# Attention with heads of 16 columns: projections of the next batch earlier in the order, heads issued in pairs, and score products on 64-row halves of the array

## The chip, the cores and the metric

One core of a Trainium2 chip runs one launch of the whole model. The metric is device time in microseconds (us). The core's engines are TensorE (PE in the rows; its weight loads PEld), VectorE (DVE), ScalarE (ACT), GpSimd (POOL) and SyncE (SP), which issues the DMAs here. Each runs its own list of instructions in order and waits on semaphores.

## The reference

Four layers, each a gated attention block and a gated mixture of experts, on 8 batches of 256 rows and 256 columns. The attention of layers 1 and 2 has 16 heads of 16 columns. With x the state, c the context:

```
n = layernorm(x)
q, k, v = n @ Wq + bq, c @ Wk + bk, c @ Wv + bv          # split into 16 heads of 16
layer 1: q, k = rotary(q), rotary(k); causal and padding masks
s = q @ k.T / 4 + mask
p = softmax(s)
x = x + tanh(gate) * (concat(p @ v) @ Wo + bo)
```

Layer 2 has no rotation and no causal mask. Layers 0 and 3 have other attention code.

## The kernel before, in words

`small_phase` (L1697) is the attention of layers 1 (`att1`, `rotary` true) and 2 (`att2`); layers 0 and 3 and the experts are not touched. The 8 batches times 16 heads are 128 steps. In step s TensorE does four things in this order: `scores` of head s+8 (L1823 to L1825 in layer 1, L1828 in layer 2), from which VectorE's `largest` (L2016) takes each row's maximum; `shifted` of head s (L1842 to L1844, L1847), the same product transposed, from which the maximum is taken off by an additional row of the operands and of which ScalarE takes the exponential (`weights_of`, L1952); the rounds of this step; and `values` of head s−1 (L1871). Scores, shifted products and outputs have two banks each, the exponentials three buffers.

The operands of a head are fp32 numbers split into high and low parts, laid side by side into 64 rows: `lay_hi` on ScalarE (L1962) and `lay_lo` on VectorE (L2030) write `qs` and `ks`, which TensorE transposes in four parts of four heads, qT and kT (L1910). ScalarE evacuates qT into `QT` (L1975), VectorE kT into `KT` (L2069). `KT` has two heads in its 128 rows. `QT` has a copy for each of the two, in which the other head's 64 rows are zero, so that each product goes over 128 rows; GpSimd's `clear` (L2166) writes the zeros at the start.

The `plan` table gives each round of batch b its step, 16(b−1) + the table's number: nT (transposes of the normalized input, L1893), q, k, v and out (projections, L94 to L96, as three products of split operands), qT and kT with their parts, mt (transposed maxima, L1914, which ScalarE copies and SyncE's DMAs put into `QT`), and OT (transposed outputs, L1918). All rounds share two banks in the order of the table. The first scores of batch b are at its number 8, its first shifted products at 16. The text counts the steps from 16(b−1), the number 0 of batch b, for other batches' rounds too: the out round of batch b−2 is at 4 there, kT part 3 of batch b−1 at −1. `lay_hi` and `lay_lo` of a batch are at its numbers 0 (q) and 2 (k).

GpSimd's list is, for each batch b: `norm(b)` (L2127), `aux(b)` (L2136, L2137: mask columns into `qs` and `ks`, which waits for kT part 3 of batch b−1), in layer 1 `rotate` of q and then k (L2146 to L2155), and `add_bias(b-2)` (L2161), which waits for VectorE's sum behind the output projection (L2076). `normalize` (L2038, L2043) divides eight heads' outputs.

Of the kernel before, what the change touches and what calls it, by code (L numbers as in the profile page):

```python
# [24 lines left out]
P = 128  # L25
B = 8
# [1670 lines left out]
def small_phase(nc, G, I, name, layer, weights, w, mask, biases, rotary):  # L1697
# [8 lines left out]
    plan = [(-4, "nT", 0), (-3, "q", 0), (-2, "k", 0), (1, "v", 0), (3, "qT", 0), (5, "kT", 0), (6, "qT", 1), (7, "kT", 1),  # L1706
            (8, "qT", 2), (10, "kT", 2), (11, "qT", 3), (15, "kT", 3), (13, "mt", 0), (17, "mt", 1), (21, "mt", 2), (25, "mt", 3),
            (26, "OT", 0), (34, "OT", 1), (36, "out", 0)]
    ROUNDS = sorted(((16 * (b - 1) + at, kind, b, part) for b in range(B) for at, kind, part in plan), key=lambda r: r[0])
    POS = {r[1:]: i for i, r in enumerate(ROUNDS)}  # L1710
    ON_ACT = ("qT", "mt")
# [8 lines left out]
    def batch_at(s, at):  # L1720
        b = (s - at) // 16 + 1
        return b if (s - at) % 16 == 0 and 0 <= b < B else None

    with ExitStack() as ctx:
# [10 lines left out]
        if rotary:  # L1735
# [5 lines left out]
            r1, r2 = sb("turn1", [P, TB, D]), sb("turn2", [P, TB, D])  # L1741
# [21 lines left out]
        n_ready, aux_done, f_raw, f_ready, laid_hi, laid_lo = (sem(n) for n in ("n_ready", "aux_done", "f_raw", "f_ready", "laid_hi", "laid_lo"))  # L1763
# [8 lines left out]
        def both(bank):  # L1772
            return bank[:, :].rearrange("p (c s) -> p c s", c=2)

# [3 lines left out]
        with nc.Block() as block:  # L1778
            @block.sync
            def _(sp):  # L1780
# [17 lines left out]
                for s in range(FIRST, LAST):  # L1798
                    for kind, b, part in rounds_at(s):
                        if kind == "mt":  # L1800
                            n = 4 * b + part
                            sp.wait_ge(mt_done, n + 1)
                            for e in range(2):
                                sp.dma_start(QT[b % 2][64 * e + 49:64 * e + 50, e, 2 * part:2 * part + 2, :].bitcast(F32),
                                             mT[n % 2][4 * e:4 * e + 4, :].bitcast(F32)).then_inc(row_in, 16)
# [4 lines left out]
            def _(pe):  # L1810
                def scores(s):
# [5 lines left out]
                    if s == H:  # L1817
                        pe.wait_ge(cleared, 2)
                    if s >= 2:
                        pe.wait_ge(m_done, s - 1)  # L1820
                    bank, q, k = s_ps[s % 2], QT[b % 2], KT[b % 2]
                    if rotary:
                        pe.matmul(bank[:, P:3 * P], ident16[:, :], tri[:, :, :], start=True, stop=False, skip_group_check=True)  # L1823
# [8 lines left out]
                def shifted(s):  # L1832
# [3 lines left out]
                    if s >= 2:  # L1836
                        pe.wait_ge(e_done, s - 1)
# [706 lines left out]
```

## Time and profile before

| | us |
|---|---|
| three runs | 3793.33, 3807.78, 3793.79; median 3793.79 |
| profiled execution | 3807.24, span 3805.2 |
| TensorE busy over the span | 2787.3 (73%) |
| VectorE, ScalarE, GpSimd busy | 2549.3, 1615.5, 1634.2 |
| attention of layer 1 | about 701 to 1092 |
| attention of layer 2 | about 1677 to 1979 |

In the rows the names of buffers stand without their numbers, "out<-in" is written and read, and x is a count. The time in square brackets is how long the engine was idle before the row and which engine and line released it. PEclk is the clock that TensorE was granted as a share of 2.4 GHz; 0.50 is 1.2 GHz.

### The profile page before, as it was taken

What the parts mean: (1) busy time and instruction counts of PE and PEld (TensorE: products, weight loads), DVE (VectorE), ACT (ScalarE), POOL (GpSimd) and SP (SyncE); (2) the same over time, 40 slices, a digit from 0 to 9 for tenths busy, and PEclk for the clock granted to TensorE, in tenths of its full rate; (3) what the DMA queues carried; (4) which work ended last, traced back from release to release, by engine and by line L of the source; (5) the groups of instructions that cost most, each with busy time, mean ns of one, the idle gap of its engine ahead of it and who ended that gap; (6) DMA issues with size and microseconds to landing.
All of it is one profiled execution on the core that took longest, in us unless ns stands there. A gap on an engine that the chain in (4) does not pass through costs nothing. (4 is left out here: it accounts for less than half of the span.)

```text
span 3805.2 us, 66554 instructions
## 1 busy us (share of the span) xinstructions
PE 2787.3 (73%) x20707; PEld 2610.0 (69%) x20708; DVE 2549.3 (67%) x4818; ACT 1615.5 (42%) x3415; POOL 1634.2 (43%) x1281
## 2 busy tenths in 40 slices
PE   5663584288867999929972788886189998498883
PEld 4551574288856999929971677776189888298883
DVE  4664597544436999955642788887567666388886
ACT  3222352133324555515531344443267666265551
POOL 0102455522203488740003666665344443317775
PEclk9786798677768999969965999999599999699997
DMA  3032686100005655530001455553200000365554
GB/s 96 23 133 100 197 248 182 52 18 12 7 30 202 209 195 200 171 97 18 18 4 70 150 156 158 157 156 117 67 12 6 11 11 1 127 208 180 189 182 126
DMA packets 244577, 408.83 MB, mean 107 GB/s; under 512 B 26656, under 2 KB 136492, under 8 KB 244384
## 3 DMA queue, kind: packets, MB, share of 16 engines
q1 hardware_dynamic: 230560, 368.89, 30.5%
q0 software_dynamic: 13824, 37.53, 3.0%
q8 instruction: 101, 1.65, 0.2%
q14 instruction: 92, 0.75, 0.1%
HBM read 327.91 MB, written 78.38 MB: 107 GB/s over the span
## 5 line engine op out<-in xcount | busy, mean ns | idle before, releaser
L500 POOL TENSOR_TENSOR moe2m_wlo<-moe2m_raw,moe2m_whi 128x768 fp32r<-128x768 f32 x184 | 344.2, 1872 | 196.5 <-ACT moe2m_whi L623 170.6
L500 POOL TENSOR_TENSOR moe1m_wlo<-moe1m_raw,moe1m_whi 128x768 fp32r<-128x768 f32 x138 | 272.4, 1980 | 159.6 <-ACT moe1m_whi L623 159.4
L500 POOL TENSOR_TENSOR moe3m_wlo<-moe3m_raw,moe3m_whi 128x512 fp32r<-128x512 f32 x184 | 249.0, 1370 | 164.6 <-ACT moe3m_whi L623 151.2
L717 DVE TENSOR_TENSOR moe2m_hlo<-moe2m_h_f,moe2m_hhi 128x256 fp32r<-128x256 f32 x184 | 283.0, 1538 | 14.1 <-issue 0.6
L1871 PE MATMUL att_o<-att_vp,att_p 128*128 128x17 f32 x1792 | 268.4, 282 | 3.1 <-ACT att_p L1952 3.1
L1871 PEld LDWEIGHTS att_o<-att_vp,att_p 128*128 128x128 f32 x1792 | 265.1, 224 | 3.7 <-ACT att_p L1952 3.5
L1952 ACT ACTIVATE att_p<-att_t 128x384 f32<-128x384 f32 (+1 forms) x256 | 139.4, 545 | 298.7 <-PE att_t L1844 161.6
L1623 POOL TENSOR_TENSOR att_p<-att_p,att_ri 128x512 f32<-128x512 f32 x128 | 132.8, 1040 | 290.7 <-DVE att_ri L1510 289.1
L587 POOL DMA_INDIRECT rows_x<-moe_n_all,moe_slot_w x144 | 144.6, 1004 | 221.8 <-POOLq L109 119.2
L94 PE MATMUL moe1m_gu<-moe1m_xThi,moe1m_whi 128*128 128x256 f32 x744 | 214.8, 289 | 8.6 <-DVE moe1m_wlo L500 7.9
L96 PE MATMUL moe1m_gu<-moe1m_xThi,moe1m_wlo 128*128 128x256 f32 x744 | 211.6, 284 | 6.5 <-issue 6.5
L717 DVE TENSOR_TENSOR moe3m_hlo<-moe3m_act,moe3m_hhi 128x256 fp32r<-128x256 f32 x248 | 202.6, 817 | 18.5
L95 PE MATMUL moe1m_gu<-moe1m_xTlo,moe1m_whi 128*128 128x256 f32 x744 | 211.9, 285 | 1.2 <-issue 1.0
L94 PE MATMUL moe2m_gu<-moe2m_xThi,moe2m_whi 128*128 128x256 f32 x736 | 211.0, 287 | 1.4 <-DVE moe2m_xTlo L677 1.4
L95 PE MATMUL moe2m_gu<-moe2m_xTlo,moe2m_whi 128*128 128x256 f32 x736 | 209.0, 284 | 0.0
L96 PE MATMUL moe2m_gu<-moe2m_xThi,moe2m_wlo 128*128 128x256 f32 x736 | 208.4, 283 | 0.0
L623 ACT ACTIVATE moe1m_whi<-moe1m_raw 128x768 fp32r<-128x768 f32 x186 | 157.9, 849 | 107.4 <-PE moe1m_yp L96 77.2
L651 ACT ACTIVATE moe2m_act<-moe2m_gu 128x256 f32<-128x256 f32 x184 | 70.9, 385 | 287.6 <-PE moe2m_gu L96 287.6
L94 PE MATMUL moe3m_yp<-moe3m_whi,moe3m_hhi 128*128 128x256 f32 x496 | 149.8, 302 | 54.3 <-DVE moe3m_hlo L717 37.4
L94 PE MATMUL moe2m_yp<-moe2m_whi,moe2m_hhi 128*128 128x256 f32 x368 | 120.2, 327 | 92.7 <-DVE moe2m_hlo L717 91.3
L715 DVE CAST moe1m_hhi<-moe1m_h_f 128x256 fp32r<-128x256 f32 x186 | 171.1, 920 | 15.6 <-issue 0.2
L658 ACT ACTIVATE moe3m_act<-moe3m_gu 128x256 f32<-128x256 f32 x248 | 95.9, 387 | 166.4 <-PE moe3m_gu L96 140.0
(631 smaller groups left out, 11111.4 us busy)
## 6 DMA issues: line engine op xcount, KB each, us to landing
moe1m_raw<-in_moe_w SPq DMA_DIRECT2D x186, 384.0 KB
moe2m_raw<-in_moe_w SPq DMA_DIRECT2D x184, 384.0 KB
moe3m_raw<-in_moe_w SPq DMA_DIRECT2D x248, 256.0 KB
moe0m_raw<-in_moe_w SPq DMA_DIRECT2D x92, 320.5 KB
rows_x<-att_zeros SPq DMA_DIRECT2D x24, 512.0 KB
moe0m_xr<-rows_x SPq DMA_DIRECT2D x46, 256.0 KB
rows_y<-moe0m_y SPq DMA_DIRECT2D x46, 256.0 KB, 2.3
moe1m_xr<-rows_x SPq DMA_DIRECT2D x31, 256.0 KB
```

Of the source, the lines that this page charges most:

```text
L94: pe.matmul(out, lhs[0], rhs[0], start=first, stop=False, **kw)
L95: pe.matmul(out, lhs[0], rhs[1], start=False, stop=False, **kw)
L96: return pe.matmul(out, lhs[1], rhs[0], start=False, stop=last, **kw)
L500: e.tensor_tensor(wlo[s][:, :], raw[s][:, 0:WW], whi[s][:, :].bitcast(F32), ALU.subtract).then_inc(w_lo_v if in_shared(i, lo, hi, c // FC) ...
L587: pool.indirect_dma_start(out=rows_x[0:ROWS, :], out_offset=bass.IndirectOffsetOnAxis(ap=slot_w[:, t, k:k + 1], axis=0), in_=n_all[:, t, : ...
L623: act.activation(whi[s][:, :], raw[s][:, 0:WW], ACT.Copy).then_inc(w_hi, 1)
L658: act.activation(h_f[c % RG][:, :], gu[c % RG][:, 0:BS], func).then_inc(act_done, 1)
L715: v.tensor_copy(hh[0][q][:, :], h_f[q][:, :])
L717: v.tensor_tensor(hh[1][q][:, :], h_f[q][:, :], hh[0][q][:, :].bitcast(F32), ALU.subtract).then_inc(h_ready, 1)
L1623: pool.tensor_tensor(p_sb[s % 4][:, :, :], p_sb[s % 4][:, :, :], ri[:, s % 4, :].rearrange("p (t o) -> p t o", o=1).broadcast_to([P, TB, S ...
L1871: mm = pe.matmul(out[:, t, g, :], p[:, at:at + P], v[:, c, h, :], start=(not rotary and g == 0 and i == 0), stop=(i == len(blocks) - 1), s ...
L1952: act.activation(p_sb[s % 3][:, :], t_ps[s % 2][:, 0:QB], ACT.Exp).then_inc(e_done, 1)
```

## The change

Projections: nT, q and k stand at −11, −10 and −9 in place of −4, −3 and −2, and most other rounds of the table move by one to three steps; the first batch has an order of its own. `lay_hi` and `lay_lo` are at −2 (q) and −1 (k) in place of 0 and 2. kT part 3 of batch b−1 is at −2 of batch b's count, and the nT round of batch b+1 at 5. The diagonal tables of layer 1 are built at s = −16 and no longer −8. VectorE rotates the queries of batch 0, GpSimd all others.

Pairs: at even s TensorE issues the scores of heads s+8 and s+9 and the shifted products of s and s+1, alternating between operands in rows 0 to 63 and rows 64 to 127 and between the two banks. It waits until both banks are free. Values are those of head s−2, the exponentials have four buffers. `QT` has no zero halves, so `clear` goes and its evacuation is one instruction.

```diff
-    plan = [(-4, "nT", 0), (-3, "q", 0), (-2, "k", 0), (1, "v", 0), (3, "qT", 0), (5, "kT", 0), (6, "qT", 1), (7, "kT", 1),
...
+    plan = [(-11, "nT", 0), (-10, "q", 0), (-9, "k", 0), (1, "v", 0), (2, "qT", 0), (5, "kT", 0), (8, "qT", 1), (9, "kT", 1),
...
+    first = {"k": -12, "v": -11, "nT": -10, "q": -9}
+    LAY = {(16 * (b - 1) + (-2 if (kind == "q") == (b > 0) else -1)): (b, kind) for b in range(B) for kind in ("q", "k")}
...
-        QT = [sb(f"QT{q}", [P, 2, H // 2, S], F32R) for q in range(2)]
+        QT = [sb(f"QT{q}", [P, H // 2, S], F32R) for q in range(2)]
...
-        p_sb = [sb(f"p{q}", [P, QB]) for q in range(3)]
+        p_sb = [sb(f"p{q}", [P, QB]) for q in range(4)]
...
+        def rotate(e, b, kind, a1, a2):
...
                     if s >= 2:
-                        pe.wait_ge(m_done, s - 1)
-                    bank, q, k = s_ps[s % 2], QT[b % 2], KT[b % 2]
+                        pe.wait_ge(m_done, s)
+                    q, k = ([y[64 * e:64 * e + 64, h // 2, :] for e in range(2)] for y in (QT[b % 2], KT[b % 2]))
                     if rotary:
...
+                        for e in range(2):
+                            pe.matmul(s_ps[e][:, P:3 * P], ident16[:, :], tri[:, :, :], start=True, stop=False, skip_group_check=True)
+                        for e in range(2):
+                            pe.matmul(s_ps[e][:, 0:2 * P], q[e][:, 0:P], k[e], start=False, stop=False, skip_group_check=True)
+                        for e in range(2):
+                            pe.matmul(s_ps[e][:, 2 * P:3 * P], q[e][:, P:S], k[e][:, 0:P], start=False, stop=True,
+                                      skip_group_check=True).then_inc(s_ready, 1)
                     else:
                         for t in range(TB):
...
+                            for e in range(2):
+                                mm = pe.matmul(s_ps[e][:, t * S:(t + 1) * S], q[e][:, t * P:(t + 1) * P], k[e], start=(t == 0), stop=True,
+                                               skip_group_check=True)
...
-                        pe.wait_ge(e_done, s - 1)
...
+                        pe.wait_ge(e_done, s)
...
-                    if 0 <= s + L < NS:
+                    if 0 <= s + L < NS and s % 2 == 0:
                         scores(s + L)
-                    if 0 <= s < NS:
+                    if 0 <= s < NS and s % 2 == 0:
                         shifted(s)
                     for r in rounds_at(s):
                         round_(*r)
-                    if 0 <= s - 1 < NS:
-                        values(s - 1)
+                    if 0 <= s - 2 < NS:
+                        values(s - 2)
...
-                    for at, kind in ((0, "q"), (2, "k")):
-                        if batch_at(s, at) is not None:
-                            lay_hi(batch_at(s, at), kind)
+                    if s in LAY:
+                        lay_hi(*LAY[s])
...
-                        for e in range(2):
-                            ins = act.activation(QT[b % 2][64 * e:64 * e + 64, e, 2 * part:2 * part + 2, :], both(bank)[64 * e:64 * e + 64], ACT.Copy)
-                        ins.then_inc(rd_act, 1)
+                        act.activation(QT[b % 2][:, 2 * part:2 * part + 2, :], both(bank), ACT.Copy).then_inc(rd_act, 1)
...
+                        if rotary and b == 0 and kind == "q":
+                            v.wait_ge(kq_done, 1)
+                            rotate(v, 0, "q", r3, r4).then_inc(q_ready, 1)
...
-                    if rotary and s == -8:
+                    if rotary and s == -16:
...
-                    if s >= 9 and (s - 9) % 8 == 0 and (s - 9) // 8 < 2 * B:
-                        normalize((s - 9) // 8)
+                    if s >= 10 and (s - 10) % 8 == 0 and (s - 10) // 8 < 2 * B:
+                        normalize((s - 10) // 8)
...
-                def clear(q):
-                    for e in range(2):
-                        pool.drain()
-                        pool.memset(QT[q][64 - 64 * e:128 - 64 * e, e, :, :].bitcast(F32), 0.0)
...
-                    if rotary:
-                        rotate(b, "q")
-                        rotate(b, "k")
...
+                    for kind in ("q", "k") if rotary else ():
+                        if b > 0 or kind == "k":
+                            pool.wait_ge(f_raw, 2 * b + (kind == "k"))
+                            rotate(pool, b, kind, r1, r2).then_inc(q_ready if kind == "q" else k_ready, 1)
                     if b >= 2:
                         add_bias(b - 2)
```

ScalarE, layer 1, at the turn to a batch. L1952 and L1980 are the exponentials, L1962 and L1990 `lay_hi` of queries (`qs`) and keys (`ks`), L1982 and L2008 the maxima of four heads. Before:

```order
L1982 ACTIVATE att1_mT0<-att1_r0 8x128
L1952 ACTIVATE att1_p0<-att1_t0 128x384
L1952 ACTIVATE att1_p1<-att1_t1 128x384
L1952 ACTIVATE att1_p2<-att1_t0 128x384
L1962 ACTIVATE att1_qs<-att1_qf 128x32x32
L1952 ACTIVATE att1_p0<-att1_t1 128x384
L1982 ACTIVATE att1_mT1<-att1_r0 8x128
L1952 ACTIVATE att1_p1<-att1_t0 128x384
L1962 ACTIVATE att1_ks<-att1_kf 128x64x16
L1987 ACTIVATE att1_OT_hi<-att1_r0 128x256
```

and in the changed kernel:

```order
L2008 ACTIVATE att1_mT0<-att1_r0 8x128
L1980 ACTIVATE att1_p2<-att1_t0 128x384
L1990 ACTIVATE att1_qs<-att1_qf 128x32x32
L1980 ACTIVATE att1_p3<-att1_t1 128x384
L1990 ACTIVATE att1_ks<-att1_kf 128x64x16
L1980 ACTIVATE att1_p0<-att1_t0 128x384
L1980 ACTIVATE att1_p1<-att1_t1 128x384
L2008 ACTIVATE att1_mT1<-att1_r0 8x128
```

Behind the copy of maxima (`mT0`) three exponentials stood ahead of the first `lay_hi`, and now one does; between the two stands one exponential and no longer two.

TensorE, layer 1, behind the last key transposes of a batch (L1910 before, L1938 after, `ks`). L1871 and L1899 are values, L1823 and L1840 the first product of scores. Before:

```order
L1910 MATMUL att1_r1<-g_identr,att1_ks 128x128 x4
L1871 MATMUL att1_o1<-att1_vp1,att1_p0 128x17 x3
L1823 MATMUL att1_s0<-att1_tri,att1_ident16 128x256
L1824 MATMUL att1_s0<-att1_KT0,att1_QT0 128x256
L1825 MATMUL att1_s0<-att1_KT0,att1_QT0 128x128
L1842 MATMUL att1_t0<-att1_dg,att1_tri 128x256
L1843 MATMUL att1_t0<-att1_QT0,att1_KT0 128x256
L1844 MATMUL att1_t0<-att1_QT0,att1_KT0 128x128
L1871 MATMUL att1_o1<-att1_vp1,att1_p1 128x17 x3
L1823 MATMUL att1_s1<-att1_tri,att1_ident16 128x256
```

and in the changed kernel:

```order
L1869 MATMUL att1_t0<-att1_QT0,att1_KT0 128x128
L1869 MATMUL att1_t1<-att1_QT0,att1_KT0 128x128
L1938 MATMUL att1_r0<-g_identr,att1_ks 128x128 x4
L1899 MATMUL att1_o1<-att1_vp0,att1_p0 128x17 x3
L1899 MATMUL att1_o1<-att1_vp0,att1_p1 128x17 x3
L1840 MATMUL att1_s0<-att1_tri,att1_ident16 128x256
L1840 MATMUL att1_s1<-att1_tri,att1_ident16 128x256
L1842 MATMUL att1_s0<-att1_KT1,att1_QT1 128x256
L1842 MATMUL att1_s1<-att1_KT1,att1_QT1 128x256
```

Two heads of values follow the transposes directly, then the scores of a pair in both banks; before, each head had scores and shifted products of its own.

TensorE, layer 1, behind the output projection (`w1_wo`), in the changed kernel. L1921 is the transpose of the normalized input (nT), L1942 that of the maxima:

```order
L94 MATMUL att1_r1<-w1_wo_hi,att1_OT_hi 128x256
L95 MATMUL att1_r1<-w1_wo_lo,att1_OT_hi 128x256
L96 MATMUL att1_r1<-w1_wo_hi,att1_OT_lo 128x256
L1899 MATMUL att1_o0<-att1_vp1,att1_p2 128x17 x3
L1942 MATMUL att1_r0<-g_ident,att1_mm0 8x128
L1938 MATMUL att1_r1<-g_identr,att1_ks 128x128 x4
L1921 MATMUL att1_r0<-g_ident,att1_n 128x128 x4
L1899 MATMUL att1_o0<-att1_vp1,att1_p3 128x17 x3
L1840 MATMUL att1_s0<-att1_tri,att1_ident16 128x256
```

The nT round of batch b+1 stands one head behind the output projection of batch b−2; before, the projection stood at 4 and this nT round at 12.

## Rows read from the trace of the kernel before

**Rows 1.** Stretches: start:end, length, busy (instructions) of PE, PEld, DVE, ACT, POOL; clock; DMA.

```profile
751.00:1092.00 341.00, 300.54 (x2179) 297.34 (x2177) 139.74 (x308) 121.30 (x251) 90.29 (x117) 0.74 0.04 11
1707.00:1979.00 272.00, 267.63 (x2162) 263.32 (x2161) 148.49 (x247) 130.88 (x251) 17.79 (x33) 0.91 0.04 13
...
841.10:879.70 38.60, 33.12 (x290) 32.80 (x289) 18.70 (x41) 15.96 (x33) 13.03 (x18) 0.87 0.05 15
879.70:931.30 51.60, 46.32 (x291) 46.21 (x289) 18.99 (x41) 16.42 (x33) 13.08 (x18) 0.64 0.03 12
1020.00:1069.00 49.00, 49.00 (x265) 49.00 (x264) 16.27 (x37) 13.20 (x29) 1.27 (x1) 0.50 0.00 1
...
1925.80:1932.60 6.80, 6.80 (x64) 6.78 (x62) 3.75 (x7) 4.09 (x9) 0.00 (x0) 1.00 0.02 3
1932.60:1946.20 13.60, 13.60 (x68) 13.53 (x67) 5.16 (x9) 3.41 (x7) 0.00 (x0) 0.50 0.01 2
```

**Rows 2.** Timeline of TensorE, layer 1: start, duration, engine, line, operation.

```profile
874.36 0.50 PE L1910 MATMUL att_r<-g_identr,att_ks 128*128 128x128 f32 x4
874.70 0.81 PE L1871 MATMUL att_o<-att_vp,att_p 128*128 128x17 f32 x6
875.35 0.27 PE L1823 MATMUL att_s<-att_tri,att_ident 128*128 128x256 bf16 x1
...
885.50 0.66 PE L1918 MATMUL att_r<-g_ident,att_o 128*128 128x128 f32 x2 [5.28 <-DVE att_o L2043]
```

**Rows 3.** Timeline of GpSimd, same stretch.

```profile
874.93 0.21 POOL L2136 CAST att_qs<-att_kq 128x16 fp32r<-128x16 f32 x1 [16.86 <-PE att_r L1910]
...
879.99 1.82 POOL L2155 TENSOR_SCALAR att_qf<-att_qf,att_kq 128x256 f32<-128x256 f32 x2 [0.18 <-issue]
...
885.02 1.27 POOL L2151 TENSOR_TENSOR att_kf<-att_turn 128x512 f32<-128x512 f32 x1
```

**Rows 4.** Timeline of VectorE and ScalarE, same stretch.

```profile
881.84 1.06 ACT L1962 ACTIVATE att_qs<-att_qf 128x1024 fp32r<-128x1024 f32 x1 [5.21 <-POOL att_qf L2155]
...
882.93 0.69 DVE L2030 TENSOR_TENSOR att_qs<-att_qf,att_qs 128x512 fp32r<-128x512 f32 x1 [6.29 <-ACT att_qs L1962]
883.54 0.55 DVE L2016 TENSOR_REDUCE att_m<-att_s 128x3 f32<-128x384 f32 x1
```

**Rows 5.** Timeline of TensorE, VectorE and GpSimd, layer 2, behind an output projection.

```profile
1781.94 1.19 PE L1871 MATMUL att_o<-att_vp,att_p 128*128 128x17 f32 x8
1782.98 0.37 PE L1828 MATMUL att_s<-att_KT,att_QT 128*128 128x256 f32 x1
...
1782.18 0.75 DVE L2076 SCALAR_TENSOR_TENSOR g_x<-att_r,att_tg,g_x 128x512 f32<-128x512 f32 x1 [2.29 <-PE att_r L96]
...
1783.14 1.28 POOL L2161 TENSOR_TENSOR g_x<-g_x,att_bo 128x512 f32<-128x512 f32 x1 [12.74 <-DVEq L2078]
1784.40 1.09 POOL L2127 TENSOR_SCALAR att_n<-g_x,att_nmean,att_rstd 128x256 f32<-128x256 f32 x2
```

**Rows 6.** Timeline of TensorE, layer 2, one head with transposes and the next.

```profile
1752.50 0.49 PE L1828 MATMUL att_s<-att_KT,att_QT 128*128 128x256 f32 x2
1752.83 0.40 PE L1847 MATMUL att_t<-att_QT,att_KT 128*128 128x256 f32 x2
1753.07 0.46 PE L1910 MATMUL att_r<-g_identr,att_ks 128*128 128x128 f32 x4
1753.36 1.03 PE L1871 MATMUL att_o<-att_vp,att_p 128*128 128x17 f32 x8
1754.24 0.49 PE L1828 MATMUL att_s<-att_KT,att_QT 128*128 128x256 f32 x2
```

**Rows 7.** Timeline of TensorE, starts of layers 1 and 2.

```profile
740.90 0.63 PE L1936 MATMUL att_o<-att_dgc,g_ones_bf 128*128 128x512 bf16 x1 [5.53 <-DVEq L2111]
...
1685.23 1.11 PE L1893 MATMUL att_r<-g_ident,att_n 128*128 128x128 f32 x4 [64.22 <-POOLq L2180]
```

**Rows 8.** Timeline of GpSimd, start of layer 2.

```profile
1681.41 3.71 POOL L2166 MEMSET att_QT<- 64x2048 f32 x2
```

More of the change, by code:

```diff
@@ L1704, in small_phase @@
     MC = 3 if rotary else 2
[L1706 to L1709 removed]
+    plan = [(-11, "nT", 0), (-10, "q", 0), (-9, "k", 0), (1, "v", 0), (2, "qT", 0), (5, "kT", 0), (8, "qT", 1), (9, "kT", 1),
+            (11, "qT", 2), (12, "kT", 2), (13, "qT", 3), (14, "kT", 3), (13, "mt", 0), (17, "mt", 1), (21, "mt", 2), (25, "mt", 3),
+            (27, "OT", 0), (35, "OT", 1), (36, "out", 0)]
+    first = {"k": -12, "v": -11, "nT": -10, "q": -9}
+    ROUNDS = sorted(((16 * (b - 1) + (first.get(kind, at) if b == 0 else at), kind, b, part) for b in range(B) for at, kind, part in plan),
+                    key=lambda r: r[0])
     POS = {r[1:]: i for i, r in enumerate(ROUNDS)}
+    LAY = {(16 * (b - 1) + (-2 if (kind == "q") == (b > 0) else -1)): (b, kind) for b in range(B) for kind in ("q", "k")}
     ON_ACT = ("qT", "mt")
@@ L1718, in rounds_at, with turn_of @@
         return [r[1:] for r in ROUNDS if r[0] == s]
[L1720 to L1722 removed]
+    def turn_of(b, kind):
+        return 2 * b + 1 + ((kind == "k") == (b > 0))
     with ExitStack() as ctx:
@@ L1740, in small_phase @@
             ind = sb("ind", [P, B, P])
-            r1, r2 = sb("turn1", [P, TB, D]), sb("turn2", [P, TB, D])
+            r1, r2, r3, r4 = (sb(f"turn{q}", [P, TB, D]) for q in range(4))
         n_sb = sb("n", [P, TB, D])
@@ L1773, in both @@
             return bank[:, :].rearrange("p (c s) -> p c s", c=2)
+        def rotate(e, b, kind, a1, a2):
+            f = qf if kind == "q" else kf
+            half = lambda y, i: y[:, :, :].rearrange("p t (h e d) -> p t h e d", e=2, d=8)[:, :, :, i, :]
+            tab = lambda q, n: cs[:, :, q, :].rearrange("p t (o d) -> p t o d", o=1).broadcast_to([P, TB, n, 8])
+            e.tensor_tensor(a1[:, :, :].rearrange("p t (h d) -> p t h d", d=8), f[:, :, :].rearrange("p t (h d) -> p t h d", d=8), tab(0, 32), ALU.mult)
+            e.tensor_tensor(half(a2, 0), half(f, 1), tab(1, 16), ALU.mult)
+            e.tensor_tensor(half(a2, 1), half(f, 0), tab(2, 16), ALU.mult)
+            e.drain()
+            ins = e.tensor_tensor(f[:, :, :], a1[:, :, :], a2[:, :, :], ALU.add)
+            if kind == "q":
+                e.drain()
+                for t in range(TB):
+                    ins = e.tensor_scalar(f[:, t, :], f[:, t, :], kq[:, b, t:t + 1], None, ALU.mult)
+            return ins
         def done(kind, b, part=0):
@@ L1836, in shifted @@
                     if s >= 2:
-                        pe.wait_ge(e_done, s - 1)
-                    bank, q, k = t_ps[s % 2], QT[b % 2], KT[b % 2]
+                        pe.wait_ge(e_done, s)
+                    q, k = ([y[64 * e:64 * e + 64, h // 2, :] for e in range(2)] for y in (QT[b % 2], KT[b % 2]))
                     if rotary:
@@ L1931, in _ @@
                 pe.wait_ge(cleared, 1)
-                for s in range(FIRST, max(LAST, NS + 2)):
+                for s in range(FIRST, max(LAST, NS + 3)):
                     if rotary and s == -7:
@@ L1993, in _ @@
                     act.drain().then_inc(tri_ready, 1)
-                for s in range(FIRST, max(LAST, NS + 2)):
+                for s in range(FIRST, max(LAST, NS + 3)):
                     if 0 <= s < NS:
```

85 lines of the change are left out of this document (34 added, 51 removed).

## The prediction, made before the changed kernel ran

> **What bounds the kernel now.** I read the stretch view first. In layer 1's attention TensorE works 300.5 of 341 us at a mean granted clock of 0.74; in layer 2's it works 267.6 of 272 us at 0.91, while VectorE, ScalarE and GpSimd have much time over [rows 1]. So TensorE sets both, and weight loads are as busy as products (263.3 beside 267.6 us). What is left over in layer 1 is one hole in each batch. In the batch of 841 to 880 us all runs at 38.6 us for 16 heads; in the next the clock is 0.64 and the batch takes 51.6 [rows 1]. Behind batch 7, from 1020 to 1069, TensorE is wholly busy and stays at 0.50. A low clock is layer 1's largest loss.
>
> The engines' timelines give the hole's chain. TensorE starts the last key transposes of a batch (kT part 3) at 874.36, and goes on at 885.50, after 5.28 us idle [rows 2]; between the two it worked. GpSimd's mask columns come at 874.93, right behind those transposes, and only then the rotation of the next queries, which ends at 879.99 + 1.82 = 881.81 [rows 3]. ScalarE lays the high half (881.84, 1.06 us), VectorE the low half (882.93, 0.69 us), and VectorE's queue holds its `largest` reductions behind this [rows 4]. So the hole is hung on kT part 3 of the batch before, by way of `aux`, and not on the projections: nine heads' more lead for q and k doesn't shorten it, since `aux(b)` still stands ahead of `rotate` on GpSimd and still waits for that part.
>
> **Part 1, the rotation (layer 1, batches 1 to 7).** In the next batch's count of the table, kT part 3 goes from −1 to −2, and the laying of q from 0 to −2. By the same durations, VectorE begins `lay_lo` of q 882.93 − 874.36 = 8.57 us after kT part 3 starts. Queued behind are `lay_lo` itself (0.61 to its successor's start), the kT copy (0.61 too, since it is as large), and `largest` (0.55 at 883.54 [rows 4]); the scores of the next pair need that reduction. That is 8.57 + 0.61 + 0.6 + 0.55 + 0.1 of signalling = 10.4 us. TensorE in the meantime has the rest of the transposes (874.70 − 874.36 = 0.34) and two heads of values (0.65 each, from 874.70 to 875.35 [rows 2]): 1.6 us. It idles 8.8 us where it idled 5.3: +3.5 us, seven times, **+25 us**. The laying of k, now at −1, makes a second, small hole: GpSimd rotates k until 885.02 + 1.27 = 886.29 [rows 3], 4.5 us more, so VectorE's next pair of reductions ends about 14.8 us after kT part 3 starts, while TensorE, on again at 10.4, has 3.7 us of products and of the v projection: 0.7 us, seven times, **+5 us**. Bounds of both: 0, if the hole only shifts with the mask columns, which come a head sooner; +40, if `lay_hi` of k (1.06 us, as that of q) holds the exponentials of the next pair too.
>
> **Part 2, a new wait for the norm (both layers, batches 3 to 7).** The normalized input's transposes (nT) of batch b+1 move from eight steps behind the output projection of batch b−2 to one step behind. GpSimd's order is bias of b−2, then norm of b+1. In layer 2 the projection's last product is over and values begin at 1781.94; VectorE adds it at 1782.18 (0.75), GpSimd adds the bias at 1783.14 and normalizes from 1784.40 for 1.09 us, so it is ready at 1785.49 [rows 5]: 3.55 us. TensorE has in that time values (1782.98 − 1781.94 = 1.04), one small transpose (0.1) and one kT round (0.29, from 1753.07 to 1753.36 [rows 6]): 1.4 us. It waits 2.1 us, in layer 1 about 2.3 as its values are shorter; ten times, **+22 us**. Before, all of this lay beside eight heads of products. Lowest 0 (a row of GpSimd could start sooner), highest 3.5 × 10 = +35.
>
> **Part 3, starts and tail.** In layer 2 GpSimd cleared the padded halves before TensorE's first transposes at 1685.23, released by GpSimd [rows 7]; that goes, 3.71 us of memsets just ahead of it [rows 8]. In layer 1 the diagonal tables held TensorE 5.53 us before 740.90; they are now built eight steps sooner, and I take 3.5 of it. Together **−7 us** (bounds 0 and −11). The values run one head later at each end, **+1 us**. The query evacuation is one ScalarE instruction and not two, and there is a fourth buffer of weights: ScalarE isn't late in these rows (its busy share is under one half in both stages), so nothing. Neither engine's queue is long enough for the two-bank waits to show: both reductions of a pair (0.55 or 0.69 each) end within the pair's values. Where a kT evacuation falls between them in layer 1 it may cost 0.3 us; it lies in front of the hole, so nothing.
>
> **Part 4, the clock.** Behind the hole at 885.50 the pair of transposes takes 0.66 us and the clock of the batch is 0.64. Behind other holes it came back, in the 38.6 us batches. The new order puts dense projections soon behind the hole (v at number 1, out at 4, q at 6, k at 7), so I expect it back more often: two of the batches at 51.6 instead of 38.6 go, 2 × 13 = 26, **−25 us** (bounds −45 and +10). The ten new waits of part 2 come ahead of a long stretch of heads in layer 2, whose clock fell at 1932.6 with no idleness ahead of it [rows 1]: one fall more of 13.6 us at half speed costs 7 us, and two of them **+12 us** (0 to +35).
>
> **Part 5, pairs on the two halves.** In layer 2 a head has two scores products and two shifted ones: 1752.83 − 1752.50 = 0.33 and 0.24 us, so 0.12 us each in a stream; its eight values products take 0.88, or 0.11 each, with 17 columns only [rows 6]. So a 128-column weight load sets the same pace as 256 moving columns. No run of before shows a product on 64 rows; nearest are these full ones. If only products overlap and loads queue, the pace of 0.12 stays and the gain is 0. If both overlap, two of four go: 0.24 us a head, 128 heads, 30 us in layer 2, and 20 in layer 1, whose products are partly of 128 columns: −50. Against it stands the change between whole array and halves: four times a pair in layer 1 (tables and triangles are whole products), twice in layer 2, 64 pairs each, 384 in all. A lone product lasts 0.37 us (1782.98 [rows 5]) against 0.12 in a stream; if each change emptied the array, 0.25 us, +96; if not, 0. I take a full gain of 50 eaten by 0.13 us a change, **0**, halfway, since no row is nearer to either end.
> The Trainium skill bears on both sides. "TensorEngine Tiling (Array Packing)", Key Properties, states that different tiles load weights and multiply in parallel, and also that changing the tiling mode drains TensorE. By the first alone the sum would fall by the 50 us, by the second alone rise by up to 96. No run of before shows either.
>
> **Sum.** The profiled execution took 3807.2 us (span 3805.2), 13 us over the median of 3793.8; as its rows carry the sum, it is made against that: 25 + 5 + 22 − 7 + 1 − 25 + 12 + 0 = +33, so 3840. Against the median it would be 3827; the upper of the three runs (3807.8) is near the profiled one. I take 3835, between the two.
>
> **Rivals.**
> - *R1, full overlap, clock as forecast.* Then −50: 3785. For it: values' rows show loads as the pace, so halves that load beside each other save all of it. Against: 384 changes of mode.
> - *R2, full overlap, and layer 1's clock holds.* Behind batch 7 the tail of 49 us at 0.50 [rows 1] would run in half, −24, and the remaining slow batch −13: about 3745 to 3750. This ends well faster. Against: the hole is longer, 8.8 us, and it was the hole that the clock fell behind at 885.50.
> - *R3, layer 2's clock falls in the heads without transposes.* Its place is the heads without transposes or projections, about half of each batch. At 1925.8 to 1932.6 the clock is 1.00 with TensorE busy throughout, then 0.50 for 13.6 us [rows 1]. So this stretch is near the edge even now; with two heads' products beside each other, fewer are in work at a time, and with the waits of part 2 there is idleness ahead. Decides from one fall in every batch on: six falls of 13.6 us at half speed cost 6 × 6.8 = 41 beyond the forecast's two: 3835 + 41 = 3876, or 3865 if the pairs still give back some 10, and up to 3890 with eight falls.
> - *R4, every change of mode empties the array.* +96 − 50 instead of 0: 3881. A lone product's 0.37 speaks for it; the modelled ends of products make it weak.
> - *The chain of part 1 isn't made longer* (the hole stays 5.3 us): 3835 − 30 = 3805, which would be no change. I give it no chance of its own; it is part of the forecast's lower edge.
> The first page's rule has a second consequence: if weights load in parallel, halves help even at 128 columns. "TensorE: Matmul & The Clock Gate", Part 3, adds that a load overlaps products in flight only where their row groups differ, which by itself speaks for R1; by this rule the time would be 3785. The trace of before agrees only in that loads of one row group keep 0.11 us apart [rows 6].
>
> **How the numbers follow.** Forecast 0.40 (own range 3805 to 3862), R3 0.25, R1 0.15, R2 0.12, R4 0.08. The range of all reaches from between R1 and R2, whose lower half is left out, to above R4 and R3: 3762 to 3892. What a measurement of this kernel can tell from no change is 0.5%, 3775 to 3813. Faster: R2 and a half of R1, 0.19. Same: the other half of R1 and the lower edge of the forecast, 0.20. Slower: the rest, 0.61.
>
> **What would show it.** Part 1: TensorE idle in front of the scores of each layer 1 batch, nearly 9 us and released by VectorE, with GpSimd's mask columns still right behind kT part 3. Part 2: ten waits of about 2 us of nT for GpSimd. Part 5: in layer 2 a head takes 1.74 us with 0.29 of transposes (1752.50 to 1754.24 [rows 6]), so a pair without them 2.9 us; 2.4 would show full overlap, 3.4 a change of mode that empties the array. R3: the granted clock of layer 2 below 0.85. Wrong would be: layer 1's hole at 5 us or less, or layer 2 shorter than 265 us.

## The result, and the profile after

The changed kernel takes 4004.74 us (median of 4 runs, 3999.05 to 4010.24) against 3800.78 for the kernel before in all its runs so far: 1.052 of it, 95% interval 1.049 to 1.055. I had said 3835 and at most 3892.

The stretch view of the changed kernel, first its attention of layer 1 and of layer 2, then a part of the latter (columns as in [rows 1]):

```profile
710.20:1159.80 449.60, 362.67 (x2308) 304.14 (x2308) 158.51 (x361) 109.10 (x234) 95.60 (x127) 0.66 0.03 9
1750.00:2168.40 418.40, 397.53 (x2272) 377.34 (x2272) 159.28 (x263) 122.50 (x233) 19.25 (x35) 0.57 0.03 10
1900.40:2002.80 102.40, 99.81 (x525) 95.82 (x525) 37.96 (x63) 28.61 (x54) 5.37 (x10) 0.50 0.04 12
```

The same stretches of the kernel before:

```profile
712.10:1091.60 379.50, 321.22 (x2307) 316.39 (x2308) 157.13 (x355) 130.49 (x266) 105.81 (x135) 0.73 0.04 11
1685.20:1978.80 293.60, 285.35 (x2272) 279.07 (x2272) 160.14 (x265) 140.38 (x265) 22.90 (x39) 0.90 0.05 14
```

Layer 1 is longer by 70 us, layer 2 by 125; the two spans differ by 192. The number of products is the same (2272 in layer 2). TensorE's time outside products grew by 29 us in layer 1 (449.6 − 362.7 against 379.5 − 321.2) and 13 us in layer 2; the other 154 us are products that take longer, at a clock of 0.66 where it was 0.73 and 0.57 where it was 0.90. For over 100 us of layer 2 the clock stands at 0.50 and TensorE is at work for 97% of that (99.81 of 102.4 us).

The chain around a hole of layer 1, in the timelines of TensorE, GpSimd and VectorE of the changed kernel:

```profile
895.37 0.54 PE L1938 MATMUL att_r<-g_identr,att_ks 128*128 128x128 f32 x4
905.82 0.59 PE L1840 MATMUL att_s<-att_tri,att_ident 128*128 128x256 bf16 x2 [8.37 <-DVE att_m L2041]
...
895.97 0.21 POOL L2166 CAST att_qs<-att_kq 128x16 fp32r<-128x16 f32 x1 [23.91 <-PE att_r L1938]
...
900.97 1.82 POOL L1790 TENSOR_SCALAR att_qf<-att_qf,att_kq 128x256 f32<-128x256 f32 x2 [0.17 <-issue]
...
903.91 0.69 DVE L2055 TENSOR_TENSOR att_qs<-att_qf,att_qs 128x512 fp32r<-128x512 f32 x1 [8.58 <-ACT att_qs L1990]
904.52 0.69 DVE L2100 CAST att_KT<-att_r 128x512 fp32r<-128x512 f32 x1
905.12 0.55 DVE L2041 TENSOR_REDUCE att_m<-att_s 128x3 f32<-128x384 f32 x1
```

The mask columns (895.97) still stand right behind the key transposes and ahead of the rotation. `lay_lo` comes 8.54 us after those transposes (8.57 forecast), the next scores 10.45 us after them (10.4 forecast), after 8.37 us idle (8.8). The waits of TensorE from 757 to 1151 us in layer 1 and, in the last line, from 1781 to 2158 in layer 2, as line waited for, us in total, times and longest:

```profile
PE att_s L1840 <- DVE att_m L2041: 50.5, 7, 8.6
PE att_r L1921 <- POOL att_n L2157: 10.3, 5, 2.1
...
PE att_r L1921 <- POOL att_n L2157: 8.0, 5, 2.1
```

The first hole of layer 1, that of batch 1, lies just ahead of this stretch and is the longest:

```profile
755.34 0.59 PE L1840 MATMUL att_s<-att_tri,att_ident 128*128 128x256 bf16 x2 [9.93 <-DVE att_m L2041]
```

The first product of layer 2 now waits for a DMA:

```profile
1749.97 0.55 PE L94 MATMUL att_r<-w_wk_hi,att_cT_hi 128*128 128x256 f32 x1 [62.38 <-DMA att_cT_lo<-ctxT_lo]
```

Before, from 751 to 1092 us, the holes made 32.5 us in all:

```profile
PE att_r L1918 <- DVE att_o L2043: 32.5, 7, 5.3
```

One by one in the timelines, these are six holes of 5.3 us (batches 2 to 7) and one wait of 0.95; batch 1 had no such hole. In the changed kernel the same six take 8.60, 8.59, 8.37, 8.60, 8.59 and 7.42 us, the seventh wait of the view is 0.35, and batch 1's 9.93 comes on top: 60 us for seven holes where six made 32. So parts 1 and 2 are there, +28 and +18 us. Now the products themselves, from TensorE's timeline in layer 2, one pair of heads at the high clock and one at the low:

```profile
1896.37 0.50 PE L1849 MATMUL att_s<-att_KT,att_QT 64*128 64x256 f32 x4
1896.71 0.40 PE L1874 MATMUL att_t<-att_QT,att_KT 64*128 64x256 f32 x4
1897.04 0.55 PE L1938 MATMUL att_r<-g_identr,att_qs 128*128 128x128 f32 x4
...
1915.74 0.79 PE L1849 MATMUL att_s<-att_KT,att_QT 64*128 64x256 f32 x4
1916.33 0.63 PE L1874 MATMUL att_t<-att_QT,att_KT 64*128 64x256 f32 x4
1916.89 1.89 PE L1899 MATMUL att_o<-att_vp,att_p 128*128 128x17 f32 x8
```

From 1893.5 to 1900.4 the granted clock is 0.99, from 1900.4 on 0.50. Eight half products take 1897.04 − 1896.37 = 0.67 us at 2.4 GHz, where eight whole ones took 2 × 0.57 [rows 6]. They do run beside each other, and still the kernel is slower by 5%.

### The profile page after: what moved, and what is told of

Its sections match the earlier page's. It is cut to its first block and busy times, and to the rows that moved or that the text cites. A ratio compares the mean times of both kernels' runs of the same rounds, so it can differ in the third digit from the quotient of the medians.

```text
span 3997.6 us, 66470 instructions
## 1 busy us (share of the span) xinstructions
PE 2949.3 (74%) x20708; PEld 2700.2 (68%) x20708; DVE 2558.2 (64%) x4824; ACT 1573.8 (39%) x3351; POOL 1613.5 (40%) x1267
## 5 line engine op out<-in xcount | busy, mean ns | idle before, releaser
L1899 PEld LDWEIGHTS att_o<-att_vp,att_p 128*128 128x128 f32 x1792 | 342.3, 284 | 5.9 <-issue 4.0
L1899 PE MATMUL att_o<-att_vp,att_p 128*128 128x17 f32 x1792 | 343.0, 330 | 0.0
L717 DVE TENSOR_TENSOR moe2m_hlo<-moe2m_h_f,moe2m_hhi 128x256 fp32r<-128x256 f32 x184 | 293.4, 1595 | 13.7
L1980 ACT ACTIVATE att_p<-att_t 128x384 f32<-128x384 f32 (+1 forms) x256 | 129.4, 541 | 356.1 <-PE att_t L1874 185.0
L2173 POOL TENSOR_TENSOR g_x<-g_x,att_bo 128x512 f32<-128x512 f32 x16 | 20.3, 1266 | 372.5 <-DVEq L2109 372.5
```

The costliest lines, as they stand in the source:

```text
L717: v.tensor_tensor(hh[1][q][:, :], h_f[q][:, :], hh[0][q][:, :].bitcast(F32), ALU.subtract).then_inc(h_ready, 1)
L1899: mm = pe.matmul(out[:, t, g, :], p[:, at:at + P], v[:, c, h, :], start=(not rotary and g == 0 and i == 0), stop=(i == len(blocks) - 1), s ...
L1980: act.activation(p_sb[s % 4][:, :], t_ps[s % 2][:, 0:QB], ACT.Exp).then_inc(e_done, 1)
```

## The experiments

Theory A: issued so, TensorE's clock falls, and the holes are the small part. Theory B: the new waits are what lowers the clock, pairs and halves are innocent. Each experiment ran beside the kernel before, whose median was 3727.9, 3727.7, 3732.6 and 3739.0 us in the four groups, so I compare ratios to it. The changed kernel did not run in these groups. Outside the two attentions its profiled execution took 3130 us and that of the kernel before beside it 3132, all the others 3044 to 3065; what made these 75 us isn't known. With them off, the changed kernel's ratio would be about 1.055 by the groups' footing, by (4004.7 − 73) / 3728, an estimate. "L1" and "L2" are the stretches from the first to the last product of the two attentions, with their granted clock.

| | ratio (interval) | L1 us, clock | L2 us, clock |
|---|---|---|---|
| before | 1 | 379.5, 0.73 | 293.6, 0.90 |
| changed | 1.052 (1.049 to 1.055) | 449.6, 0.66 | 418.4, 0.57 |
| e1 pairs, 128 rows | 1.033 (1.025 to 1.041) | 419.2, 0.72 | 381.5, 0.73 |
| e2 table only | 1.006 (1.002 to 1.010) | 398.4, 0.72 | 325.6, 0.85 |
| e3 halves, single heads | 1.091 (1.087 to 1.095) | 532.3, 0.55 | 474.1, 0.56 |
| e4 changed, values 64 wide | 1.011 (1.007 to 1.014) | 395.2, 0.81 | 326.9, 0.84 |
| e5 before, values 64 wide | 0.984 (0.981 to 0.987) | 332.0, 0.87 | 272.4, 0.98 |
| e6 before, 128 wide | 0.983 (0.980 to 0.986) | 330.5, 0.90 | 271.9, 0.98 |
| e7 changed, two moves | 1.020 (1.015 to 1.025) | 352.5, 0.78 | 384.3, 0.62 |
| e8 the same, 128 wide | 0.980 (0.977 to 0.983) | 308.7, 0.94 | 286.8, 0.96 |
| e9 table, two moves | 0.975 (0.971 to 0.979) | 278.3, 0.95 | 310.0, 0.89 |
| e10 the same, 128 wide | 0.975 (0.973 to 0.976) | 289.1, 0.95 | 286.6, 0.97 |
| e11 halves, single, 128 wide | 1.019 (1.017 to 1.021) | 433.4, 0.81 | 314.7, 0.97 |
| e12 before, 32 wide | 0.984 (0.982 to 0.986) | 349.0, 0.81 | 272.8, 0.98 |
| e13 pairs, 128 rows, two moves | 1.000 (0.996 to 1.003) | 332.5, 0.83 | 359.0, 0.75 |
| e14 the same, 128 wide | 0.981 (0.977 to 0.986) | 303.9, 0.95 | 296.3, 0.97 |

**e1, pairs without halves.**

```diff
-        QT = [sb(f"QT{q}", [P, H // 2, S], F32R) for q in range(2)]
+        QT = [sb(f"QT{q}", [P, 2, H // 2, S], F32R) for q in range(2)]
...
-                    q, k = ([y[64 * e:64 * e + 64, h // 2, :] for e in range(2)] for y in (QT[b % 2], KT[b % 2]))
+                    q, k = [QT[b % 2][:, e, h // 2, :] for e in range(2)], [KT[b % 2][:, h // 2, :] for e in range(2)]
```

> The changed kernel with its order, its pairs and its table, but each score product again over all 128 rows, with the zero halves of QT back (QT of twice the size, GpSimd's clears, the query evacuation in two instructions). Theory A (the two 64-row products run beside each other, TensorE has fewer columns in work at a time, and the clock falls for that): layer 2's clock is back at about 0.9 and its attention at 270 to 280 us instead of 376; layer 1's hole and norm waits stay; in all about 3840 to 3870. Theory B (the waits of the new table lower the clock): the clock stays near 0.56 in layer 2, and as the overlap is gone too, the time goes up to 4030 to 4060.

3845.6 us is what theory A said, but only as the kernel before took 3727.9 in this group and not 3800.8; the ratio is 1.033. The clock of layer 2 went to 0.73 and not to 0.9, half of the way, and its attention to 381.5 us and not to 270 to 280. Halves are a part of the fall, not all.

**e2, the table alone**, heads one at a time (e1 with the former `scores`, `shifted` and lag of values):

```diff
-                    if 0 <= s + L < NS and s % 2 == 0:
+                    if 0 <= s + L < NS:
                         scores(s + L)
```

> The changed kernel with its table alone: heads issued one at a time as before, 128-row products with zero halves, values one head behind. Theory A: holes of about 7.5 us in layer 1 and ten norm waits of about 1.9 us stay, the clock of layer 2 is about 0.9; 3820 to 3860. Theory B: clock of layer 2 near 0.56, 3950 or more. Either way the part of the 204 us that the table alone makes is read from it.

Ratio 1.006: of the 5.2%, the table makes 0.6, the pairs' order 2.7 and the halves 1.9 (2.2 if the changed kernel's ratio is taken as 1.055).

**e3, halves alone.**

```diff
-                    bank, q, k = s_ps[s % 2], QT[b % 2], KT[b % 2]
+                    r = slice(64 * (h % 2), 64 * (h % 2) + 64)
+                    bank, q, k = s_ps[s % 2], QT[b % 2][r], KT[b % 2][r]
```

> The kernel before, table and order unchanged, but each head's score and shifted products over its 64 rows alone (no zero halves, no clears, one query evacuation). Heads still come one at a time, so hardly any two products stand beside each other. Theory A in the form 'running side by side lowers the clock': same time as before less the 4 us of the start, 3790 to 3800, product pace 0.12 us as before. Theory A2 in the form 'half the array's rows at work lowers the clock': layer 2's clock falls as in the changed kernel, 3900 or more. Theory C (a change between whole array and halves costs time): over 3830 with the clock unchanged.

The strongest result. A stretch of its layer 2, and TensorE's timeline of one head at the low clock:

```profile
1805.00:2250.00 445.00, 444.86 (x2159) 413.05 (x2160) 151.55 (x244) 119.43 (x222) 17.76 (x33) 0.56 0.03 8
```

```profile
1895.10 0.79 PE L1827 MATMUL att_s<-att_KT,att_QT 64*128 64x256 f32 x2
1895.69 0.62 PE L1847 MATMUL att_t<-att_QT,att_KT 64*128 64x256 f32 x2
1896.25 0.75 PE L1910 MATMUL att_r<-g_identr,att_qs 128*128 128x128 f32 x4
```

TensorE is busy for 444.9 of 445 us, without a hole or a new wait, and its clock is 0.56. Theory B falls for layer 2: going over 64 rows in these products is enough to lower it (A2), with heads one at a time and no two products beside each other. It also brings changes between the whole array and a half, and no run parts the two. Two half products of the same rows take 0.59 us, as long as four that alternate (1915.74 to 1916.33 above, at the same clock), so the overlap needs alternating halves.

**e4, wider values**, a change of what TensorE streams and nothing else:

```diff
-        vp = [sb(f"vp{q}", [P, KC, H, dh + 1]) for q in range(2)]
+        VW = 64
+        vp = [sb(f"vp{q}", [P, KC, H, VW]) for q in range(2)]
...
-                        mm = pe.matmul(out[:, t, g, :], p[:, at:at + P], v[:, c, h, :], start=(not rotary and g == 0 and i == 0),
+                        to = (8 * t + g) * (dh + 1)
+                        mm = pe.matmul(o_ps[half % 2][:, to:to + VW], p[:, at:at + P], v[:, c, h, :], start=(not rotary and g == 0 and i == 0),
```

> The changed kernel with the moving operand of each values product 64 columns wide instead of 17: 16 value columns, the ones, and 47 columns of zeros that are added to the same output bank. If the clock follows how many columns TensorE streams, and a weight load sets the pace of these products: pace still 0.11 us at the high clock, clock of layer 2 1.0 and of layer 1 over 0.85, and 3780 to 3830. If the clock follows idle time or the halves themselves: clock unchanged, 4000. If 64 columns take longer than a load: slower than 4005 by up to 1792 x 0.1 = 180 us.

1.052 became 1.011 with all waits in place (the holes of layer 1 from 757 us on made 50.5 us and make 51.6, the norm waits there 10.3 and 10.4). The clocks, 0.81 and 0.84, stayed under the 0.85 and 1.0 that I had expected. Eight values products of 64 columns at the high clock:

```profile
1757.14 1.00 PE L1901 MATMUL att_o<-att_vp,att_p 128*128 128x64 f32 x8
1757.97 0.27 PE L1944 MATMUL att_r<-g_ident,att_mm 128*8 128x128 f32 x1
```

0.83 us for eight, where eight of 17 columns took 0.88 [rows 6]: in layer 2, 47 more columns cost nothing.

**e5, e6 and e12, wider values in the kernel before** (the diff of e4 with `VW` of 64, 128 and 32).

> The kernel before with values products 64 columns wide (47 of them zeros), all else unchanged. If what TensorE streams sets its clock, the low stretches of layer 1 (clock 0.73 over its 380 us) and layer 2 (0.90 over 294 us) go for the most part: 40 to 90 us less than the kernel before. If idle time behind the rotation sets it in layer 1, layer 1's clock stays near 0.73 and the gain is under 30 us. If 64 columns take longer than the load, slower.

> As the one with 64 columns, with 128. If the pace of these products is set by the weight load alone, 0.11 us as with 64 columns, and the clock in both attentions still higher: 10 to 30 us less than with 64. If 128 columns of this type stream for longer than a load: pace of 0.2 us and 1792 x 0.1 = 150 us or so slower.

> The kernel before with values 32 columns wide. 17 columns ran at 0.73 and 0.90 in layers 1 and 2, 64 at 0.87 and 0.98. If the clock follows the columns by degrees, 32 lie between: about 0.78 and 0.95, ratio 0.990. If only the last step counts, as 17 (ratio 1.00); if a little is enough, as 64 (0.984).

All three beat the kernel before, by 1.6 to 1.7%, 60 us or so. In layer 1 the clock rises by steps with the width (0.73, 0.81, 0.87, 0.90); in layer 2 32 columns already reach 0.98. My expected ratio of 0.990 for 32 columns was too modest; the degrees showed in layer 1 alone. And 128 columns gave nothing clear over 64, where I had expected 10 to 30 us. The kernel with 128, layers 1 and 2:

```profile
692.70:1023.20 330.50, 271.71 (x2307) 264.78 (x2308) 159.32 (x355) 128.78 (x266) 109.78 (x138) 0.90 0.04 13
1593.00:1864.90 271.90, 263.69 (x2272) 257.46 (x2272) 160.08 (x263) 140.18 (x265) 22.94 (x39) 0.98 0.05 15
```

**e7, the causes of parts 1 and 2 taken away** in the changed kernel's GpSimd order.

```diff
+                    if b >= 3:
+                        add_bias(b - 3)
                     if b == 0:
                         pool.wait_ge(kq_done, 1)
-                    aux(b)
                     for kind in ("q", "k") if rotary else ():
...
-                    if b >= 2:
-                        add_bias(b - 2)
-                for b in (B - 2, B - 1):
+                    aux(b)
+                for b in (B - 3, B - 2, B - 1):
```

> The changed kernel with two moves in GpSimd's order: the rotation of q and k ahead of the mask columns, so that it no longer waits for the last key transposes, and the norm of the next batch ahead of the bias of batch b-3. If my parts 1 and 2 have the right causes, the seven holes (50.5 us together) shrink to under 10 us and the ten norm waits (18 us) to nothing: 50 to 65 us less than the changed kernel, the clock unchanged near 0.57 in layer 2. If the holes set the clock, it recovers too and the gain is over 100 us. If the holes hang on something else (the laying on ScalarE behind exponentials, for one), they stay over 4 us each.

1.052 became 1.020, some 120 us; the two stretches are shorter by 97 and 34 us. From batch 2 on the holes are 1.6 us each, and the norm waits are gone:

```profile
PE att_s L1840 <- DVE att_m L2041: 10.1, 7, 1.6
```

Batch 1's hole is 2.5 us and no longer 9.9, so the seven are 12 us instead of 60. That is 48 + 18 us of waits, about half of what the stretches lost. The other half is products: TensorE's busy time falls from 362.7 to 322.9 us in layer 1 (clock 0.66 to 0.78), where it was 321.2 before the change, and from 397.5 to 369.7 in layer 2 (0.57 to 0.62), where it was 285.4. So the waits account for nearly all of the longer products of layer 1 and for a quarter of those of layer 2. The gain is that of my second case, over 100 us, though most of layer 2's clock stays gone.

**e9 and e10, table and moves, no pairs, no halves**, with 17 and 128 columns: e2 with the diff of e7, and e10 with that of e4 too.

> The changed kernel's table with both moves in GpSimd's order, heads one at a time, 128-row products: no pairs, no halves, 17-column values. If the table is worth something once its two waits are gone: the hole of layer 1 under 2 us, 30 to 60 us less than the kernel before (ratio 0.985 to 0.992). If the table's dense places lower the clock of layer 2 by themselves (0.85 with the table alone), the gain there is lost again: ratio 0.995 to 1.005.

> The same with values 128 columns wide. If holes and columns are the two things that set the time, and the pairs and halves are worth nothing at the high clock (their 33.3 us for 16 heads of layer 2 against 32.5 of the kernel before with 128 columns), this beats all so far: layer 1 about 300 us, layer 2 about 272, ratio 0.970 to 0.977. If pairs and halves do help layer 1, it stays behind them at 0.980.

These are the fastest of all, 0.975 for both; their medians are 86 and 93 us below that of the kernel before. I had expected 0.985 at best for e9. With the rotation no longer behind the mask columns, layer 1 falls from 379.5 to 278.3 us in the one with 17 columns:

```profile
690.70:969.00 278.30, 255.54 (x2308) 247.01 (x2308) 164.82 (x361) 127.39 (x266) 101.22 (x129) 0.95 0.05 15
1537.50:1847.50 310.00, 293.86 (x2272) 284.83 (x2272) 159.85 (x264) 141.88 (x265) 23.36 (x39) 0.89 0.04 13
```

In layer 1, 128 columns take it up again to 289.1 us at the same clock, and give 23 us in layer 2; both intervals hold 0.975. So the width isn't quite free in layer 1: at a clock of 1.00, six values products take 0.65 us with 17 columns (846.01 to 846.66 in e9) and 0.66 to 0.74 with 128 (849.78 to 855.78 in e10).

The new table itself costs layer 2 some 15 us, whatever the clock: 310.0 against 293.6 us with 17 columns (0.89 and 0.90), 286.6 against e6's 271.9 with 128 (0.97 and 0.98). Eight of the 15 lie ahead of the first shifted product, which comes 22.6 us after the first product of all in e6 and 30.5 in e10.

**e8, e13 and e14, pairs and halves at either clock.** e8 is e7 with `VW = 128`, e13 is e1 with both moves, e14 that with 128 columns; the edit of e8 beside e7:

```diff
-        vp = [sb(f"vp{q}", [P, KC, H, dh + 1]) for q in range(2)]
+        VW = 128
+        vp = [sb(f"vp{q}", [P, KC, H, VW]) for q in range(2)]
```

> The changed kernel with both moves and values 128 columns wide: half-array products beside each other, no holes, a fuller stream. If columns and idle time both count and halves count for half: clock 0.95 or more in both attentions, and faster than the kernel before, 3620 to 3680 where that one takes 3728. If halves as such keep the clock low: layer 2 under 0.7 and no faster than the kernel before.

> The changed kernel with both moves in GpSimd's order and 128-row products in its pairs (zero halves back), 17-column values. Heads one at a time gave ratio 0.9752 to the kernel before, pairs on halves 1.0198. If the pairs' order alone lowers the clock (more values products in a row): 1.00 to 1.02, layer 2's clock 0.75 or less. If the waits were what lowered it with the pairs, and the halves do the rest: 0.975 to 0.985, layer 2's clock 0.85 or more.

> The same with values 128 columns wide, so that the clock is near 1 in all of this family: against heads one at a time (0.9746) it gives the pairs' own waits, against pairs on halves (0.9801) what the halves give or take at the high clock. If a change between whole and half array costs about 0.17 us and overlap gives back 0.24 us a head in layer 2 and less in layer 1, halves are 15 us or so dearer: this one 0.975 to 0.978. If halves are worth their overlap, it is over 0.985.

With 17 columns the steps single heads, pairs, pairs on halves (e9, e13, e7) are 0.975, 1.000, 1.020, and layer 2's clock 0.89, 0.75, 0.62. With 128 columns (e10, e14, e8) they are 0.975, 0.981, 0.980 and 0.97, 0.97, 0.96. Nearly all that pairs and halves cost is clock. At the high clock halves against whole rows are worth nothing that the intervals tell (e8 against e14: layer 1 is 5 us longer, layer 2 10 us shorter). For e14 I had set 0.975 to 0.978, or over 0.985; it fell between. The timelines of layer 2 say why, a pair of e14 (whole rows) and then one of e8 (halves):

```profile
1701.46 0.71 PE L1852 MATMUL att_s<-att_KT,att_QT 128*128 128x256 f32 x4 [1.38 <-DVE att_mm L2047]
1702.01 0.64 PE L1877 MATMUL att_t<-att_QT,att_KT 128*128 128x256 f32 x4
1702.49 1.06 PE L1903 MATMUL att_o<-att_vp,att_p 128*128 128x128 f32 x8
1703.38 0.27 PE L1946 MATMUL att_r<-g_ident,att_mm 128*8 128x128 f32 x1
```

```profile
1715.55 1.12 PE L1901 MATMUL att_o<-att_vp,att_p 128*128 128x128 f32 x8
1716.60 0.50 PE L1850 MATMUL att_s<-att_KT,att_QT 64*128 64x256 f32 x4
1716.94 0.40 PE L1875 MATMUL att_t<-att_QT,att_KT 64*128 64x256 f32 x4
1717.27 0.53 PE L1940 MATMUL att_r<-g_identr,att_ks 128*128 128x128 f32 x4
```

Four shifted products take 0.48 us whole and 1717.27 − 1716.94 = 0.33 in halves, while eight values products ahead of a half product take 1.05 us where they take 0.89 ahead of a whole one: the change into halves costs 0.16. The way back shows no price: the half products ahead of it take 0.33 us, those ahead of more halves 0.34. In layer 1, with four changes in a pair, two of them into halves, scores and shifted products of a pair take 852.72 to 854.00 = 1.28 us whole and 893.98 to 895.37 = 1.39 in the changed kernel:

```profile
852.72 0.38 PE L1843 MATMUL att_s<-att_tri,att_ident 128*128 128x256 bf16 x2
...
854.00 0.50 PE L1942 MATMUL att_r<-g_identr,att_qs 128*128 128x128 f32 x4
```

```profile
893.98 0.38 PE L1840 MATMUL att_s<-att_tri,att_ident 128*128 128x256 bf16 x2
...
895.37 0.54 PE L1938 MATMUL att_r<-g_identr,att_ks 128*128 128x128 f32 x4
```

There the overlap is eaten by the changes, and more. The Trainium skill, "TensorEngine Tiling (Array Packing)", Key Properties, has both: tiles load and multiply in parallel, and a change of the tiling mode drains TensorE. These rows agree with the first; of the second they show the way into halves alone, at 0.16 us.

**e11, halves with single heads and 128 columns** (the diffs of e3 and e4, `VW = 128`).

> The kernel before with 64-row products one head at a time and values 128 columns wide. With 17 columns that kernel ran at a clock of 0.55 and 9% slower than before. If rows at work and columns streamed add up in what the clock follows, 128 columns lift it to 0.9 and over: ratio 0.99 to 1.01, with the changes between whole and half array as what is left of the loss (256 in layer 2 at 0.1 to 0.2 us). If 64-row products as such keep the clock low, it stays near 0.56 and the ratio over 1.06.

1.091 became 1.019 (0.99 to 1.01 expected), layer 2's clock 0.97: with values of 128 columns between them, the half-row products of layer 2 no longer go with a low clock. In layer 1 it stays at 0.81. Layer 2's 314.7 us against e6's 271.9 at nearly the same clock (0.97 and 0.98) is what changes into halves without overlap cost, 43 us for 128 heads or 0.33 us a head.

## Why the prediction was wrong

- **Part 1 (rotation)**: the mechanism and the chain right to 0.1 us; +28 us measured in waits where I summed +30. That the totals are this near is in part luck. I had counted seven times 3.5 us, and it is 3.1 us in each of six batches and 9.9 in batch 1, which had no hole to lengthen. The second hole, for k, is not there: its reductions end 14.65 us after the key transposes as forecast (14.8), but TensorE has products until 913.28, at 1.2 GHz. By e7 the part costs more than its waits, as it also lowers layer 1's clock.
- **Part 2 (norm)**: right, 18.3 us of 22.
- **Part 3 (starts)**: wrong in sign. Layer 2's first product now waits for the context's DMA (1749.97, after 62.38 us idle, where it was 64.22 [rows 7]); 1.8 us of the 3.7 came. The 5.53 us wait for the diagonal tables is gone. But from the first product to the first shifted one layer 1 takes 46.3 us and no longer 39.0, where batch 1's hole now lies, and layer 2 takes 31.5 and no longer 22.5; by e10 against e6 that isn't the clock. I had no term for the new order of the first rounds, and no run changed it alone.
- **Part 4 (clock)**: the step that failed. I had −25 us for layer 1 and +12 (at most +35) for layer 2; products got longer by 41 and 112 us. I argued that dense projections behind the hole would bring the clock back, and counted falls one by one; in fact the clock stood low for 100 us on end. All terms beside the clock came to +46 in the forecast, and TensorE's time outside products grew by 41. What lowered the clock, by the runs: products on 64 rows (e3, 0.90 to 0.56 in layer 2), the pairs' order (e9 to e13, 0.89 to 0.75) and the new waits (e7, layer 1 above all), all of them with values of 17 columns; with 128 columns the same order on halves ran at 0.94 and 0.96 (e8). The warning was in [rows 1]: a clock of 0.50 with TensorE busy for all of 13.6 us means that being busy isn't enough to keep it high here, and I took that as an odd event.
- **Part 5 (halves)**: the net 0 right at the high clock (e8 against e14), and by luck: it was a midpoint between prices that no row had. By the rows above the overlap gives back about 38 us and not 50 (64 pairs at (0.55 + 0.48) − (0.34 + 0.33) = 0.36 us in layer 2 and 1.28 + 2 × 0.17 − 1.39 = 0.23 in layer 1), and only the 192 changes into halves cost something, about 0.17 us each or 33 (0.16 in layer 2; in layer 1 two triangle products take 0.31 us ahead of halves and 0.14 ahead of whole rows). Both sums are estimates. That the pairs' order alone costs 0.6% there (e10 to e14) I had at nothing: "Neither engine's queue is long enough for the two-bank waits to show" is wrong there: in e14 the scores at 1701.46 wait 1.38 us for a reduction, and 13.3 us in ten such waits of layer 2. In the changed kernel, at its low clock, it nearly held: one wait of 2.0 us from 1781 on.
- **R3** was the right rival, at 0.25, and layer 2's clock fell well below its sign of 0.85. Its reason holds in part: e3 shows that halves lower the clock with no two heads beside each other. Its price was half of what came (53 us with the forecast's 12, where layer 2's products took 112 more): I let it decide from one fall a batch and ended it at 3890. Its range should have reached what it costs when the clock stays low, from [rows 1]: 272 us at 0.91 are 247 at 1 and 495 at 0.50.

What stays open: why pairs of whole rows lower the clock (0.89 to 0.75 in layer 2, e9 to e13). More values products in a row is the difference in the order, but no run changed this alone, and the pairs also bring waits for two banks (10.1 us in e13's layer 2, 1.1 in e9's). Open too is whether it is the 64 rows or the changes between whole and half array that lower the clock in e3.

## What to carry to other kernels

If TensorE is busy throughout and its clock is 0.50, look at what it streams: widening the moving operand where a weight load sets the pace costs little, and in the kernel before it was worth 1.7%. Where the clock is high already it gives nothing (e9 to e10, layer 1). Halves of the array need both products beside each other, few changes into halves, and a clock that holds: at the high clock they were worth 10 us in layer 2 with one such change a pair, and cost 5 in layer 1 with two. When a chain runs through a queue of another engine, reorder the queue (two moves on GpSimd: 3%) before moving the work ahead.

## What the runs showed of the hardware

- Values products with a 128-row weight load and 17, 64 or 128 moving columns take 0.10 to 0.11 us each in layer 2 at 2.4 GHz. Layer 1's granted clock in the kernel before was 0.73, 0.81, 0.87 and 0.90 with 17, 32, 64 and 128 columns.
- With score products on 64 rows and values of 17 columns the clock was 0.56 over 445 us in which TensorE was busy throughout (e3); with values of 128 columns it was 0.97 in layer 2 and 0.81 in layer 1 (e11).
- Half products overlap in full when they alternate between halves, and not at all on the same half (0.59 us for four and for two at 1.2 GHz). A change into halves costs 0.16 us at 2.4 GHz.
